# Reordering the instruction queues of a software-pipelined MoE and fast-weight stage

## Chip, cores and metric

One core of one Trainium2 chip runs the kernel. The metric is the device time of one execution in microseconds (us). The engines are named as in the profile: PE (TensorE, matmuls; PEld its weight loads), DVE (VectorE), ACT (ScalarE), POOL (GpSimd) and SP (SyncE).

## What is computed

A decoder of two layers on 64 sequences of 64 tokens with 128 channels, 4096 tokens in all. Only the third and fourth of its six steps matter here, layer 0's experts and layer 1's "attention", a fast-weight step:

```python
def _L0_ffn_ref(hidden_states, w_red, wg, W1, b1, W2, b2):     # 8 experts of 256, one per token
    gates = softmax((x @ w_red) @ wg_n.T); scores = max(gates); idx = argmax(gates)
    h = gelu((x @ W1[idx]) + b1[idx]); o = (h @ W2[idx] + b2[idx]) * scores

def _L1_attn_ref(...):               # 16 heads of 64; a sequence of 64 tokens is one chunk
    lr = sigmoid(xk @ theta + tb); eta = token_eta * (lr / HD)
    Z1 = xk @ W + bb; x_hat = (Z1 - mean) / std; y = g * x_hat + be
    gxh = (y - (xv - xk)) * g
    grad_x = (HD * gxh - gxh.sum() - x_hat * (gxh * x_hat).sum()) / (HD * std)
    Wn, bn = W - (eta * xk).T @ grad_x, bb - (eta * grad_x).sum()
    Zq = xq @ Wn + bn;  out = xq + g * (Zq - mean) / std + be;  return out @ wo

x = x + _L0_ffn_ref(_layernorm(x), ...)      # ln3, experts (moe0)
x = x + _L1_attn_ref(_layernorm(x), ...)     # ln4, fast weights (fw)
```

All is float32. The step before these two ends in a dense layer whose output (`dense_T`) the same stage of the kernel adds to x.

## The kernel before

The kernel runs three stages one after the other: a first one with two attentions and a recurrent layer (to about 1000 us of the span), the middle stage of this case (about 1001 to 1936 us), and a last one with attentions, a dense layer and experts. The change touches the middle stage alone, in `phase_c` from L2670 to L2940.

The 4096 tokens are eight groups g of 512, a group is four tiles t of 128 tokens. Each engine has its queue written out by hand as one loop over g from -1 to 8, and the helpers that it calls wait on semaphores by absolute count, so that an order on one engine can be changed by moving a line. The loop is a software pipeline: in period g the engines finish the output of group g-1 (y), do the fast weights of group g, and choose and run the experts of group g+1. A helper whose group is outside 0 to 7 does nothing.

In a period these parts follow one another, by the names of the helpers (their engine is the last word of the name):

- Start: `y_first_tensor` and `y_tensor` (L2214 to L2226, nine products into bank 6) finish group g-1. Meanwhile `sum_scalar` (L2102), `sum_back_tensor` (L2116) and `experts_added_vector` (L2125) bring the experts' sum of group g back to tokens and add it to x. ln4 follows: `moments_of` (L2140, L2143), `rstd_of` (L2150, L2152), `unit_of` (L2162), `turn_of` (L2170) and `fast_input_scalar` (L2179), which gives xT. `keep_gpsimd` (L2131) stores x.
- Rates: `rates_tensor` (L2186), `rates_in_vector` (L2194), `rates_exp_scalar` (L2200) and `rates_vector` (L2206 to L2210), the learning rates eta.
- Heads: 16 products `head_tensor` (L2428) over three banks, each copied by `head_scalar` (L2434): the queries and keys. A product waits until the one three before it is copied.
- Gradient of each tile t: `z_tensor` (L2441, L2442) makes Z1, `z_square_scalar` (L2461), `z_var_vector` (L2466) and `z_rstd_scalar` (L2471, L2474) its norm, `z_unit_vector` (L2486) x_hat. On POOL `gain_gpsimd` (L2504) multiplies it; `t_tensor` makes the target, `grad_vector` (L2513) adds the two, `grad_mean_vector` (L2518) and, behind POOL's `grad_unit_gpsimd` (L2523), `grad_dot_vector` (L2528) sum up, `grad_means_vector` (L2536) scales. `rate_vector` (L2544), `grad_less_mean_vector` (L2550), POOL's `grad_along_gpsimd` (L2556), `grad_less_vector` (L2563) and `step_vector` (L2569) finish the step. Two tiles share buffers in turn (t % 2).
- Query of each tile: `key_query_tensor` (L2583, banks 4 and 5) with the copy `key_query_scalar` (L2593); `zq_tensor` (L2441, L2442) and `zq_step_tensor` (L2616) accumulate Zq in banks 6 and 7; `zq_square_scalar` (L2627), `zq_var_vector` (L2632), `zq_rstd_scalar` and `zq_unit_vector` (L2644) normalise it; `zq_turn_tensor` (L2655, banks 4 and 5 again) and `zq_turned_scalar` (L2661) turn it. zq of tile t waits for zq_unit of tile t-1, as both use banks 6 and 7, and key_query of tile t (2 and 3) for the turned copy of tile t-2.
- Choice for group g+1: `hidden_gpsimd` (L2254) copies the dense output, `hidden_turn_tensor` (L2262) turns it, `hidden_added_vector` (L2271) adds it to x; ln3; `choice_input_scalar` (L2277), `choice_reduce_tensor` (L2282), `choice_reduced_scalar` (L2288), `choice_logits_tensor` (L2295), then small DVE instructions in `choice_best_vector` (L2303, L1917 to L1925, L2307), `choice_exp_scalar` (L2313), `choice_weights_vector` (L2319 to L2323) and `choice_parts_vector` (L2333, L2336).
- Experts of group g+1: `weights_turn_tensor` (L2349), `weights_turned_scalar` (L2358), `biases_tensor` (L2364), and for each of eight experts `weight_rows_tensor` (L2374), two `expert_input_tensor` (L2387), `expert_gelu_scalar` (L2397), `expert_weighted_vector` (L2405) and `expert_output_tensor` (L2413). An input product waits for the gelu two before it, an output product for its weighted hidden half, a row for the last use of the row before. Before the gelus ACT loads a table (L2109).

All the waits are in the helpers; those that the prediction's steps touch most are these (`at` is the count of the group):

```python
def key_query_tensor(pe, S, k, t):   # t 0: fw_heads_sb of all 16; t 1: fw_A of tile 0
        pe.wait_ge(S["fw_turned_sb"], at("fw_turned_sb", k, t - 1))      # t 2 and 3
def zq_tensor(pe, S, k, t):
        pe.wait_ge(S["fw_unit2"], at("fw_unit2", k, t))                  # t 1 to 3
def zq_step_tensor(pe, S, k, t):
    pe.wait_ge(S["fw_A"], at("fw_A", k, t + 1))
    pe.wait_ge(S["fw_step"], at("fw_step", k, t + 1))
```

Of the kernel before, what the change touches and what calls it, by code (L numbers as in the profile page):

```python
# [1729 lines left out]
def phase_c(m, w):  # L1730
# [937 lines left out]
    with ExitStack() as sems:  # L2668
        S = Signals(nc, sems)
        with nc.Block() as block:  # L2670
            @block.tensor
            def _(pe):
                for g in range(-1, GROUPS + 1):
                    y_first_tensor(pe, S, g - 1)
# [13 lines left out]
                    z_tensor(pe, S, g, 1)  # L2688
# [12 lines left out]
                    choice_logits_tensor(pe, S, g + 1)  # L2701
# [4 lines left out]
                    z_tensor(pe, S, g, 2)  # L2706
# [26 lines left out]
                    weight_rows_tensor(pe, S, g + 1, 1)  # L2733
                    expert_output_tensor(pe, S, g + 1, 0, 0)
                    expert_input_tensor(pe, S, g + 1, 2, 0)
                    expert_output_tensor(pe, S, g + 1, 0, 1)
                    expert_input_tensor(pe, S, g + 1, 2, 1)
                    expert_input_tensor(pe, S, g + 1, 3, 0)
                    expert_output_tensor(pe, S, g + 1, 1, 0)
                    weight_rows_tensor(pe, S, g + 1, 2)  # L2740
                    expert_input_tensor(pe, S, g + 1, 3, 1)
                    expert_output_tensor(pe, S, g + 1, 1, 1)
# [18 lines left out]
                    expert_output_tensor(pe, S, g + 1, 5, 0)
                    weight_rows_tensor(pe, S, g + 1, 7)
                    expert_output_tensor(pe, S, g + 1, 5, 1)
                    expert_output_tensor(pe, S, g + 1, 6, 0)
                    expert_output_tensor(pe, S, g + 1, 6, 1)
# [775 lines left out]
```

## Time and profile before

| what | us |
|---|---|
| median of 3 runs (lowest, highest) | 2452.38 (2451.78, 2454.27) |
| the profiled execution's own time | 2457.08 |
| its span in the profile | 2455.4 |
| busy in the span: PE, DVE, ACT, POOL | 2013.9, 1627.3, 1136.9, 687.3 |

The profiled execution is one run by itself: its time is 4.7 us above the median, and its span is 1.7 us shorter than its time. Busy shares are means over three stages with different limits, so a change in one stage is read from that stage's own rows: a table by stretch of time, the waits by engine and releaser, and the timeline of each engine in one period of the loop.

### The profile page before, as it was taken

To read this page: it belongs to the slowest core of one execution; us is meant where nothing else is said; L and a number is where in the kernel's file an instruction comes from. 1 tells how busy PE (TensorE), PEld (TensorE's weight loads), DVE (VectorE), ACT (ScalarE), POOL (GpSimd) and SP (SyncE) were. 2 spreads that over 40 slices of the span, in tenths; PEclk is the share of its full clock that TensorE was granted. 3 is DMA by queue.
4 is the path that set the end of the run, shared out by engine and by line. 5 is a ranking of instruction groups with operands and counts; after the bars stand their busy time and mean duration, and the time that the engine had idled before them with its cause. 6 is when DMAs were issued, how large, how long until landed. Compare 5 with 4: busy or idle time off the path is not lost. (4 is left out here: it accounts for less than half of the span.)

```text
span 2455.4 us, 38656 instructions
## 1 busy us (share of the span) xinstructions
PE 2013.9 (82%) x15025; PEld 1225.2 (50%) x15025; DVE 1627.3 (66%) x3304; ACT 1136.9 (46%) x1971; POOL 687.3 (28%) x425
## 2 busy tenths in 40 slices
PE   2677788778878998689999989898989558888897
PEld 1455565566556877344444444444444334444443
DVE  3587888878753545575849485766757357677673
ACT  1576677667643443244444444444444223444342
POOL 0574476457631001031415142222324100000000
PEclk9977777887677998799999999999999669999999
DMA  2000000000003200000000000000000000000000
GB/s 73 1 8 8 6 4 8 8 6 4 8 1 89 71 1 1 0 1 1 1 1 1 1 1 1 1 1 1 1 1 1 5 9 9 9 9 9 9 5 9
DMA packets 40533, 23.56 MB, mean 10 GB/s; under 512 B 17648, under 2 KB 36896, under 8 KB 40352
## 3 DMA queue, kind: packets, MB, share of 16 engines
q1 hardware_dynamic: 40352, 21.10, 3.2%
q8 instruction: 120, 1.97, 0.3%
q14 instruction: 61, 0.50, 0.1%
HBM read 18.99 MB, written 2.10 MB: 9 GB/s over the span
## 5 line engine op out<-in xcount | busy, mean ns | idle before, releaser
L2405 DVE TENSOR_TENSOR arena<-arena,lower_banks 128x512 f32<-128x512 f32 x128 | 84.4, 685 | 145.2 <-PE lower_banks L2374 99.9
L3001 ACT ACTIVATE arena<-lower_banks,moe_b 128x512 f32<-128x512 f32 x128 | 87.9, 686 | 135.9 <-PE lower_banks L2991 126.3
L449 ACT ACTIVATE arena<-upper_banks 128x512 f32<-128x512 f32 x192 | 107.4, 593 | 88.6 <-PE upper_banks L420 56.9
L2397 ACT ACTIVATE arena<-lower_banks,moe_b 128x512 f32<-128x512 f32 x128 | 87.1, 687 | 122.7 <-PE lower_banks L2413 94.1
L2387 PE MATMUL lower_banks<-hid_w,moe_w 128*128 128x512 f32 x256 | 140.0, 641 | 1.0 <-DVE fw_b L2486 1.0
L562 POOL TENSOR_TENSOR score_mha<-score_mha,row_max_mha 128x1024 f32<-128x1024 f32 x64 | 121.7, 1908 | 57.4 <-DVE row_max_mha L500 57.4
L420 PE MATMUL upper_banks<-ident,score_mha 128*128 128x128 f32 x512 | 109.6, 362 | 32.0 <-ACT arena L449 16.8
L2413 PE MATMUL lower_banks<-arena,moe_w 128*128 128x512 f32 x256 | 125.9, 593 | 0.0
L3017 PE MATMUL upper_banks<-arena,moe_w 128*128 128x512 f32 x256 | 124.6, 595 | 0.0
L2991 PE MATMUL lower_banks<-c_xT,moe_w 128*128 128x512 f32 x256 | 123.4, 599 | 0.0
L3010 DVE TENSOR_TENSOR arena<-arena,lower_banks 128x512 f32<-128x512 f32 x128 | 86.6, 683 | 49.6 <-ACT arena L3001 47.7
L420 PEld LDWEIGHTS upper_banks<-ident,score_mha 128*128 128x128 f32 x512 | 78.8, 185 | 70.0 <-issue 34.7
L2441 PE MATMUL upper_banks<-fw_zq,c_xT 128*128 128x512 f32 x128 | 76.7, 684 | 36.5 <-DVE fw_zq_sb L2644 36.5
L2131 POOL TENSOR_TENSOR x_all<-x_cur,fw_beo 128x512 f32<-128x512 f32 x8 | 10.2, 1278 | 343.7 <-DVE x_cur L2125 343.7
L2434 ACT ACTIVATE arena<-upper_banks 128x512 f32<-128x512 f32 x128 | 76.4, 597 | 50.5 <-PE upper_banks L2428 50.5
L490 POOL TENSOR_TENSOR score_lor<-causal,aux 128x1024 f32<-128x1024 f32 x32 | 90.6, 2831 | 3.8 <-ACT aux L538 3.8
L554 POOL TENSOR_TENSOR aux<-aux,score_lor 128x1024 f32<-128x1024 f32 x32 | 82.5, 2577 | 29.0 <-ACT aux L528 28.8
L546 ACT ACTIVATE score_mha<-score_mha 128x1024 f32<-128x1024 f32 x64 | 67.1, 1054 | 48.5 <-POOL score_mha L562 48.3
L2627 ACT ACTIVATE fw_sqq<-upper_banks 128x1024 f32<-128x1024 f32 x32 | 32.8, 1025 | 102.2 <-PE upper_banks L2616 101.9
L2387 PEld LDWEIGHTS lower_banks<-hid_w,moe_w 128*128 128x128 f32 x256 | 48.9, 205 | 58.5 <-issue 43.7
L500 DVE TENSOR_REDUCE row_max_mha<-score_mha 128x16 f32<-128x1024 f32 x64 | 77.1, 1214 | 1.1
L2413 PEld LDWEIGHTS lower_banks<-arena,moe_w 128*128 128x128 f32 x256 | 49.2, 192 | 54.3 <-issue 52.3
(465 smaller groups left out, 5233.2 us busy)
## 6 DMA issues: line engine op xcount, KB each, us to landing
ctx_cur<-in_ctx_dram SPq DMA_DIRECT2D x16, 256.0 KB, 3.0
moe_w<-in_L_ffn_W_dram SPq DMA_DIRECT2D x2, 1024.0 KB
out_dram<-arena SPq DMA_DIRECT2D x8, 256.0 KB, 2.4
arena<-in_mask_Bx1x1xS_ff_dram SPq DMA_DIRECT2D x16, 64.0 KB, 2.7
arena<-in_L_xattn_lstm_w_dram SPq DMA_DIRECT2D x1, 512.0 KB, 5.1
hid_w<-in_L_xattn_ffn_w_dram SPq DMA_DIRECT2D x2, 256.0 KB, 3.1
hid_w<-in_L_xattn_w_dram SPq DMA_DIRECT2D x2, 256.0 KB
fw_q<-in_L_attn_wq_dram SPq DMA_DIRECT2D x1, 512.0 KB
```

The lines of the kernel that those rows point to most:

```text
L420: tr = nc.tensor.transpose(pair[2][:, p * P:(p + 1) * P], score[stream][:, u % ring[stream], 2 * p:2 * p + 2, :], ident[:, :])
L449: nc.scalar.activation(PT[:, 4 * half:4 * half + 4, :], pair[2][:, 512 * half:512 * half + 512].rearrange("k (p q) -> k p q", p=4), ACT.Copy)\
L490: nc.gpsimd.tensor_tensor(sc, bcast(causal[:, :], 1, H), ax, ALU.subtract).then_inc(S["lor_masked"], 1)
L562: nc.gpsimd.tensor_tensor(sc, sc, bcast(row_max[stream][:, u % ring[stream], :], 2, SEQ), ALU.subtract)\
L2387: nc.tensor.matmul(bank(i % 2), w["moe0_w1"][:, e, c * P:(c + 1) * P], expert_xT, start=True, stop=True)\
L2397: nc.scalar.activation(expert_hid[:, e % 2, c, :], bank(i % 2), ACT.Gelu, bias=w["moe0_b1"][:, e, c:c + 1])\
L2405: nc.vector.tensor_tensor(expert_hid[:, e % 2, c, :], expert_hid[:, e % 2, c, :], bank(ROW_BANK), ALU.mult)\
L2413: nc.tensor.matmul(bank(SUM_BANK), w["moe0_w2"][:, i, :], expert_hid[:, e % 2, c, :], start=False, stop=(i == E * EC - 1)).then_inc(S["moe ...
L2991: nc.tensor.matmul(bank(i % 2), w["moe1_w1"][:, e, c * P:(c + 1) * P], xT[:, :], start=True, stop=True)\
L3001: nc.scalar.activation(plan.hid[:, e % plan.ring, c, :], bank(i % 2), ACT.Relu, bias=w["moe1_b1"][:, e, c:c + 1])\
L3010: nc.vector.tensor_tensor(hid, hid, bank(ROW_BANK), ALU.mult).then_inc(S["moe1_scaled"], 1)
L3017: nc.tensor.matmul(bank(4), w["moe1_w2"][:, i, :], plan.hid[:, e % plan.ring, c, :], start=False, stop=(i == E * EC - 1)).then_inc(S["moe1 ...
```

## The change

The diff moves lines within the four queues of the middle stage. No helper, tile, semaphore or count changes, and the last stage is the same text in both kernels. On PE:

```diff
 for g in range(-1, GROUPS + 1):
+    hidden_turn_tensor(pe, S, g + 1)
     y_first_tensor(pe, S, g - 1)
...
     y_tensor(pe, S, g - 1, (6, 7))
+    z_tensor(pe, S, g, 0)
     rates_tensor(pe, S, g)
-    z_tensor(pe, S, g, 0)
     y_back_tensor(pe, S, g - 1)
-    hidden_turn_tensor(pe, S, g + 1)
+    turn_of(pe, S, "ln3", g + 1, CHOICE_BANK)
     t_tensor(pe, S, g, 0)
     head_tensor(pe, S, g, 0)
+    z_tensor(pe, S, g, 1)
+    choice_reduce_tensor(pe, S, g + 1)
     head_tensor(pe, S, g, 1)
...
     t_tensor(pe, S, g, 1)
+    z_tensor(pe, S, g, 2)
     head_tensor(pe, S, g, 4)
+    choice_logits_tensor(pe, S, g + 1)
...
     head_tensor(pe, S, g, 15)
-    z_tensor(pe, S, g, 2)
     key_query_tensor(pe, S, g, 0)
...
     zq_step_tensor(pe, S, g, 1)
+    t_tensor(pe, S, g, 3)
     zq_turn_tensor(pe, S, g, 0)
-    t_tensor(pe, S, g, 3)
-    expert_input_tensor(pe, S, g + 1, 0, 0)
     key_query_tensor(pe, S, g, 2)
     zq_tensor(pe, S, g, 2)
     zq_step_tensor(pe, S, g, 2)
+    weights_turn_tensor(pe, S, g + 1)
     zq_turn_tensor(pe, S, g, 1)
-    weights_turn_tensor(pe, S, g + 1)
-    expert_input_tensor(pe, S, g + 1, 0, 1)
     key_query_tensor(pe, S, g, 3)
-    weight_rows_tensor(pe, S, g + 1, 0)
-    biases_tensor(pe, S, g + 1)
     zq_tensor(pe, S, g, 3)
     zq_step_tensor(pe, S, g, 3)
     zq_turn_tensor(pe, S, g, 2)
+    weight_rows_tensor(pe, S, g + 1, 0)
+    expert_input_tensor(pe, S, g + 1, 0, 0)
+    biases_tensor(pe, S, g + 1)
+    expert_input_tensor(pe, S, g + 1, 0, 1)
     zq_turn_tensor(pe, S, g, 3)
```

The 28 other expert products and seven rows behind that are interleaved in another order. On ACT:

```diff
     fast_input_scalar(act, S, g)
+    rstd_of(act, S, "ln3", g + 1)
     y_scalar(act, S, g - 1)
+    z_square_scalar(act, S, g, 0)
+    choice_input_scalar(act, S, g + 1)
     rates_exp_scalar(act, S, g)
-    z_square_scalar(act, S, g, 0)
     z_rstd_scalar(act, S, g, 0)
+    z_square_scalar(act, S, g, 1)
     head_scalar(act, S, g, 0)
+    z_rstd_scalar(act, S, g, 1)
...
+    choice_reduced_scalar(act, S, g + 1)
     head_scalar(act, S, g, 3)
+    z_square_scalar(act, S, g, 2)
     head_scalar(act, S, g, 4)
+    z_rstd_scalar(act, S, g, 2)
...
     head_scalar(act, S, g, 8)
+    choice_exp_scalar(act, S, g + 1)
...
     zq_square_scalar(act, S, g, 1)
+    zq_rstd_scalar(act, S, g, 1)
     zq_turned_scalar(act, S, g, 0)
-    zq_rstd_scalar(act, S, g, 1)
...
     zq_square_scalar(act, S, g, 2)
+    weights_turned_scalar(act, S, g + 1, 0)
     zq_turned_scalar(act, S, g, 1)
```

and the turned copy of tile 3 goes from behind the second gelu to ahead of the last. On DVE:

```diff
     experts_added_vector(dve, S, g)
+    hidden_added_vector(dve, S, g + 1)
     moments_of(dve, S, "ln4", g, x_cur, "moe0_added")
     unit_of(dve, S, "ln4", g, x_cur, "ln3", g)
+    moments_of(dve, S, "ln3", g + 1, x_next, "dense_added")
+    unit_of(dve, S, "ln3", g + 1, x_next, "ln4", g)
     rates_in_vector(dve, S, g)
+    z_var_vector(dve, S, g, 0)
+    y_added_vector(dve, S, g - 1)
+    z_unit_vector(dve, S, g, 0)
     rates_vector(dve, S, g)
...
     rate_vector(dve, S, g, 0)
     grad_vector(dve, S, g, 0)
+    z_var_vector(dve, S, g, 1)
     grad_mean_vector(dve, S, g, 0)
     z_unit_vector(dve, S, g, 1)
     grad_dot_vector(dve, S, g, 0)
     grad_means_vector(dve, S, g, 0)
+    rate_vector(dve, S, g, 1)
     grad_less_mean_vector(dve, S, g, 0)
     grad_vector(dve, S, g, 1)
+    z_var_vector(dve, S, g, 2)
+    grad_less_vector(dve, S, g, 0)
+    choice_best_vector(dve, S, g + 1)
+    grad_dot_vector(dve, S, g, 1)
+    z_unit_vector(dve, S, g, 2)
     grad_mean_vector(dve, S, g, 1)
     step_vector(dve, S, g, 0)
     grad_means_vector(dve, S, g, 1)
+    choice_weights_vector(dve, S, g + 1)
     grad_less_mean_vector(dve, S, g, 1)
+    choice_parts_vector(dve, S, g + 1)
     grad_less_vector(dve, S, g, 1)
...
     grad_means_vector(dve, S, g, 2)
+    z_unit_vector(dve, S, g, 3)
     grad_less_mean_vector(dve, S, g, 2)
-    rate_vector(dve, S, g, 3)
-    z_unit_vector(dve, S, g, 3)
     zq_var_vector(dve, S, g, 1)
...
     grad_dot_vector(dve, S, g, 3)
+    rate_vector(dve, S, g, 3)
     grad_means_vector(dve, S, g, 3)
+    zq_var_vector(dve, S, g, 2)
     grad_less_mean_vector(dve, S, g, 3)
-    zq_var_vector(dve, S, g, 2)
     zq_unit_vector(dve, S, g, 2)
```

(the lines that only leave their old place are left out of the DVE and ACT parts). On POOL:

```diff
-    keep_gpsimd(pool, S, g)
-    hidden_gpsimd(pool, S, g + 2)
     gain_gpsimd(pool, S, g, 0)
...
+    gain_gpsimd(pool, S, g, 2)
     grad_along_gpsimd(pool, S, g, 1)
-    gain_gpsimd(pool, S, g, 2)
...
     gain_gpsimd(pool, S, g, 3)
+    keep_gpsimd(pool, S, g)
     grad_unit_gpsimd(pool, S, g, 3)
+    hidden_gpsimd(pool, S, g + 2)
     grad_along_gpsimd(pool, S, g, 3)
```

## Rows read from the trace of the kernel before

**Rows 1.** Table by stretch: start:end, us, busy (instructions) PE, PEld, DVE, ACT, POOL, clock, DMA.
```profile
1389.80:1503.20 113.40, 104.91 (x786) 54.45 (x785) 78.72 (x111) 48.95 (x80) 32.77 (x14) 0.97 0.00 1
```

**Rows 2.** PE's waits, 1163 to 1843 us: us in all, times, longest.
```profile
PE upper_banks L2441 <- DVE fw_zq_sb L2644: 25.6, 12, 2.6
PE upper_banks L2655 <- DVE fw_zq_sb L2644: 19.2, 6, 3.2
```

**Rows 3.** Timeline of PE, one period: start, us, instruction, [idle before <- releaser].
```profile
1395.09 0.60 PE L2170 MATMUL lower_banks<-ident,x_norm 128*128 128x128 f32 x4
...
1440.16 1.60 PE L2441 MATMUL upper_banks<-fw_zq,c_xT 128*128 128x512 f32 x2 [2.63 <-DVE fw_zq_sb L2644]
...
1452.66 1.12 PE L2441 MATMUL upper_banks<-fw_zq,c_xT 128*128 128x512 f32 x2 [1.25 <-DVE fw_zq_sb L2644]
...
1463.09 1.02 PE L2441 MATMUL upper_banks<-fw_zq,c_xT 128*128 128x512 f32 x2
...
1467.41 1.09 PE L2655 MATMUL upper_banks<-ident,fw_zq_sb 128*128 128x128 f32 x8
1471.69 1.97 PE L2655 MATMUL upper_banks<-ident,fw_zq_sb 128*128 128x128 f32 x8 [3.19 <-DVE fw_zq_sb L2644]
...
1475.85 0.38 PE L2374 MATMUL lower_banks<-cwT_parts,sel 96*128 96x512 bf16 x1
...
1501.51 1.02 PE L2218 MATMUL upper_banks<-c_xT,fw_qo 128*128 128x512 f32 x2
```

**Rows 4.** Timeline of DVE in that period.
```profile
1398.24 0.22 DVE L2194 TENSOR_TENSOR fw_eta<-upper_banks,fw_theta_b 128x64 f32<-128x64 f32 x1 [4.51 <-PE upper_banks L2186]
...
1402.69 0.68 DVE L2271 TENSOR_TENSOR ctx_cur<-x_all,upper_banks 128x512 f32<-128x512 f32 x1
...
1404.53 0.86 DVE L2140 BATCH_NORM_STATS2 ln_stats<-ctx_cur 128x6 f32<-128x128 f32 x4
...
1405.59 1.49 DVE L2544 TENSOR_TENSOR fw_small<-fw_eta,fw_small 128x16 f32<-128x16 f32 x1
...
1410.67 1.11 DVE L2162 TENSOR_SCALAR x_norm<-ctx_cur,ln_moments,ln_rstd 128x128 f32<-128x128 f32 x4
...
1414.23 1.16 DVE L2536 TENSOR_SCALAR fw_small<-fw_small 128x32 f32<-128x32 f32 x1
...
1416.56 1.21 DVE L2513 TENSOR_TENSOR fw_o<-fw_gbe,lower_banks 128x1024 f32<-128x1024 f32 x1
...
1418.95 2.85 DVE L2563 TENSOR_TENSOR arena<-arena 128x1024 f32<-128x1024 f32 x1
...
1444.95 1.87 DVE L2544 TENSOR_TENSOR hid_w<-fw_eta,hid_w 128x16 f32<-128x16 f32 x1
...
1461.63 1.22 DVE L2644 TENSOR_TENSOR fw_zq_sb<-upper_banks,fw_small 128x1024 f32<-128x1024 f32 x1 [0.62 <-ACT fw_small L2474]
```

**Rows 5.** Timeline of DVE (first fence line) and POOL in the first stage.
```profile
317.96 1.42 DVE L481 SCALAR_TENSOR_TENSOR aux<-score_lor 128x1024 f32<-128x1024 f32 x1
...
318.26 3.34 POOL L554 TENSOR_TENSOR aux<-aux,score_lor 128x1024 f32<-128x1024 f32 x1
...
323.43 2.36 POOL L554 TENSOR_TENSOR aux<-aux,score_lor 128x1024 f32<-128x1024 f32 x1
```

**Rows 6.** Timeline of POOL in the period of rows 3.
```profile
1390.90 1.27 POOL L2131 TENSOR_TENSOR x_all<-x_cur,fw_beo 128x512 f32<-128x512 f32 x1 [42.35 <-DVE x_cur L2125]
1401.39 1.08 POOL L2254 COPY h_cur<-seq_x 128x512 f32<-128x512 f32 x1 [9.22 <-PE upper_banks L2262]
...
1415.46 2.94 POOL L2556 TENSOR_TENSOR arena<-arena,fw_small 128x1024 f32<-128x1024 f32 x1
```

**Rows 7.** Timeline of ACT in that period.
```profile
1447.34 1.02 ACT L2661 ACTIVATE arena<-upper_banks 128x1024 f32<-128x1024 f32 x1
```

**Rows 8.** Table by stretch, four us behind X in two periods.
```profile
1440.10:1444.10 4.00, 3.94 (x6) 1.27 (x6) 3.86 (x6) 0.78 (x3) 1.55 (x2) 0.57 0.00 0
1780.20:1784.20 4.00, 3.93 (x60) 2.46 (x62) 3.86 (x6) 0.78 (x3) 1.56 (x2) 1.00 0.00 0
```

More of the change, by code:

```diff
@@ L2732, in _ @@
                     expert_input_tensor(pe, S, g + 1, 1, 1)
-                    weight_rows_tensor(pe, S, g + 1, 1)
                     expert_output_tensor(pe, S, g + 1, 0, 0)
                     expert_input_tensor(pe, S, g + 1, 2, 0)
+                    weight_rows_tensor(pe, S, g + 1, 1)
                     expert_output_tensor(pe, S, g + 1, 0, 1)
                     expert_input_tensor(pe, S, g + 1, 2, 1)
+                    expert_output_tensor(pe, S, g + 1, 1, 0)
                     expert_input_tensor(pe, S, g + 1, 3, 0)
-                    expert_output_tensor(pe, S, g + 1, 1, 0)
                     weight_rows_tensor(pe, S, g + 1, 2)
+                    expert_output_tensor(pe, S, g + 1, 1, 1)
                     expert_input_tensor(pe, S, g + 1, 3, 1)
-                    expert_output_tensor(pe, S, g + 1, 1, 1)
+                    expert_output_tensor(pe, S, g + 1, 2, 0)
                     expert_input_tensor(pe, S, g + 1, 4, 0)
@@ L2750, in _ @@
                     expert_output_tensor(pe, S, g + 1, 3, 0)
+                    weight_rows_tensor(pe, S, g + 1, 4)
                     expert_input_tensor(pe, S, g + 1, 5, 1)
-                    weight_rows_tensor(pe, S, g + 1, 5)
                     expert_output_tensor(pe, S, g + 1, 3, 1)
@@ L2755, in _ @@
                     expert_output_tensor(pe, S, g + 1, 4, 0)
+                    weight_rows_tensor(pe, S, g + 1, 5)
+                    expert_output_tensor(pe, S, g + 1, 4, 1)
                     expert_input_tensor(pe, S, g + 1, 6, 1)
-                    expert_output_tensor(pe, S, g + 1, 4, 1)
+                    expert_output_tensor(pe, S, g + 1, 5, 0)
+                    weight_rows_tensor(pe, S, g + 1, 6)
+                    expert_output_tensor(pe, S, g + 1, 5, 1)
                     expert_input_tensor(pe, S, g + 1, 7, 0)
-                    weight_rows_tensor(pe, S, g + 1, 6)
+                    expert_output_tensor(pe, S, g + 1, 6, 0)
+                    weight_rows_tensor(pe, S, g + 1, 7)
                     expert_input_tensor(pe, S, g + 1, 7, 1)
[L2761 to L2764, printed above, removed]
                     expert_output_tensor(pe, S, g + 1, 6, 1)
@@ L2839, in _ @@
                     expert_gelu_scalar(act, S, g + 1, 7, 0)
+                    zq_turned_scalar(act, S, g, 3)
                     expert_gelu_scalar(act, S, g + 1, 7, 1)
@@ L2849, in _ @@
+                    z_unit_vector(dve, S, g, 0)
                     rates_vector(dve, S, g)
-                    y_added_vector(dve, S, g - 1)
-                    z_var_vector(dve, S, g, 0)
-                    hidden_added_vector(dve, S, g + 1)
-                    z_unit_vector(dve, S, g, 0)
-                    moments_of(dve, S, "ln3", g + 1, x_next, "dense_added")
                     rate_vector(dve, S, g, 0)
                     grad_vector(dve, S, g, 0)
+                    z_var_vector(dve, S, g, 1)
@@ L2857, in _ @@
                     grad_mean_vector(dve, S, g, 0)
-                    z_var_vector(dve, S, g, 1)
-                    unit_of(dve, S, "ln3", g + 1, x_next, "ln4", g)
                     z_unit_vector(dve, S, g, 1)
-                    rate_vector(dve, S, g, 1)
                     grad_dot_vector(dve, S, g, 0)
                     grad_means_vector(dve, S, g, 0)
+                    rate_vector(dve, S, g, 1)
                     grad_less_mean_vector(dve, S, g, 0)
                     grad_vector(dve, S, g, 1)
+                    z_var_vector(dve, S, g, 2)
@@ L2872, in _ @@
                     grad_less_mean_vector(dve, S, g, 1)
[L2873 removed]
+                    choice_parts_vector(dve, S, g + 1)
                     grad_less_vector(dve, S, g, 1)
[L2875 removed]
+                    rate_vector(dve, S, g, 2)
                     step_vector(dve, S, g, 1)
[L2877 to L2879 removed]
```

24 lines of the change are left out of this document (removed).

## The prediction

> **What bounds the kernel now.** The change reaches only the middle stage, so I read the table by stretch first: of a period of some 113 us, PE is busy 104.9 and DVE 78.7, at a granted clock of 0.97 [rows 1]. PE looks like the bound, but the list of PE's waits over six periods says what its pauses end on: the tile `fw_zq_sb`, which DVE writes in L2644, 25.6 and 19.2 us, 7.5 a period [rows 2]. In time order [rows 3] the period ends with the next y_first at 1501.51. Tile t's zq product can start only when DVE has finished zq_unit of tile t-1. These starts, which I call X, Y and Z, are 1440.16, 1452.66 and 1463.09; the last turn starts at 1471.69 after 3.19 us of idle. From the second row of experts (1475.85) to the end PE has no wait. So two stretches alternate: DVE sets the pace from about 1401 to 1463, PE sets it for the rest. An instruction moved on PE ahead of X, Y or Z gains nothing by itself; one that leaves the DVE stretch can.
>
> **The port between DVE and POOL** decides what a DVE instruction costs there. An elementwise DVE instruction with both inputs in SBUF took 1.22 us alone, but grad_less of tile 0 took 2.85, because gain and grad_unit ran on POOL [rows 4]. grad_vector of tile 1 (1416.56), which reads PSUM, took 1.21 while POOL's grad_along ran from 1415.46 [rows 4, 6]. The trace also shows who goes first when both want the port: L481 on DVE finished at 319.38, and the POOL instruction placed at 318.26 took 3.34 instead of 2.36 us [rows 5]. A DVE instruction that already waits goes ahead of POOL's next.
>
> **Start of a period: 0 us.** hidden_turn (0.43 us of PE) moves to the front, where it only fills; hidden_added (0.68), ln3's moments (1.06 from the start of L2140 to that of rate0) and ln3's unit (1.11, of which some 1.0 until the next one starts) go into DVE's 4.51 us idle ahead of rates_in [rows 4]. hidden_added now delays ln4 by 0.7 us, but ln4's turn at 1395.09 comes behind six y products [rows 3], about 1.4 us after its input; if that cover were gone the 0.7 would count whole.
>
> **DVE up to the means of tile 0: -0.8 us.** Of 2.76 us that leave, the moments lay under POOL's gain of tile 0: rate0 behind them took 1.49 us, held until 1407.08 [rows 4], and grad0 needs that gain in any case. The three rates instructions, ahead of z_var0 before (some 1.0 us), come in at this place. So until grad0 nothing is won, and I place it 0.2 us later. After it ln3's unit is missing, 1.0 us; grad_means0, held by gain1 until 1415.39 [rows 4], ends near 1414.6: -0.8.
>
> **From there to X: 0 to +1.2 us, taken +0.6.** The same work is in another order, with rate1 added. Before, the port cost 1.63 us on grad_less0 [rows 4], and by the same reading some 3.5 on the choice's small instructions. Now I count 1.9 on grad_less0, 1.35 on step0 (behind gain2), 1.6 on the choice weights (behind grad_along1): 4.9 against some 5.1. What the trace doesn't settle is rate1, put between means0 and grad_less_mean0. Before, grad_less_mean0 took the port at once and grad_along waited: 2.94 us, some 1.05 of it the wait [rows 6]. If POOL now gets in behind rate1, grad_less_mean0 waits out 1.9 us and X is 1.2 later. The Trainium skill, "SBUF — State Buffer", section "Who interferes with whom", says that issue order decides who blocks and the holder keeps the pair for its whole instruction; grad_less0's 2.85 us agrees. By that rule grad_along gets in and the whole +1.2 stands, which makes the final time about 2442. I take the middle, since no row shows this meeting.
>
> **X to Y: -1.1 us.** rate3 cost 1.87 us here, held by grad_along2 [rows 4]; it leaves. z_unit3, which reads PSUM, takes its place, and grad_less_mean2 then waits some 0.7 us for the same POOL instruction. Bounds: -1.7 (no wait) and +0.2 (if POOL's keep, 1.27 us [rows 6], got ahead of grad_less2). **Y to Z: -0.1 us.** grad_less_mean3 now stands behind grad_along3 (0.9), but it covers the 0.62 us that zq_unit2 waited for its rstd [rows 4]. Bounds -0.6 and +1.0 (the hidden copy, 1.08 us [rows 6], which moves behind grad_unit3).
>
> **PE in these stretches: 0 us.** New idle opens: key_query 0 comes right behind the last head and waits for its copy (about 0.85), and key_query 2 and 3 come right behind a turn and wait for ACT's 1.02 us copy [rows 7], as t_3 and two expert inputs no longer stand between. In ACT's queue, rstd of z2 and the choice's exponent stand ahead of later head copies, which holds the heads by 1 to 2.5 us. All ends before X, Y and Z by 0.4, 0.8 and 2.2 us in my count. The first is thin.
>
> **The tail: -0.75 us.** The expert inputs, weight row and biases that had filled other waits (0.86, 0.86, 0.22 and 0.96 us) now fill the 3.19 us ahead of the last turn, all but about 0.3. The wait itself ends no sooner: DVE and ACT still take 4.3 us from the last zq product. What goes is the clock's fall behind it: from the turn to the second row PE took 4.16 us. At the full clock it is 2.65: the turn before took 1.09 against 1.97, 0.93 until the next instruction starts, and an expert product takes 0.86 (28 of them and seven rows of 0.22 fill the 25.66 us from 1475.85 to 1501.51) [rows 3]. That is 1.5 us. But 2.2 us of idle ahead of Z is new. After 2.63 us of idle at X the granted clock was 0.57 over four us in this period, near the lower of its two levels (1.2 and 2.4 GHz), but 1.00 in another period after as long a wait [rows 8]. So half, between 0 and -1.5. The 25.66 us of experts stay; ACT's last turned copy (1.02) moves among the gelus, where ACT idles 1 to 2 us.
>
> **Once:** in the period before group 0, both first inputs move behind the row, and nothing hides them there: two products of 0.86 to 1.0 us, +1.8. In group 7, which has no experts behind it: -1. No DMA moves; SP's queue is empty in this stage.
>
> **Sum.** Seven periods of -0.8 + 0.6 - 1.1 - 0.1 - 0.75 = -2.15 give -15.1; with +1.8 and -1, -14.3. The profiled execution took 2457.08 us (span 2455.4), so 2442.8; against the median of 2452.38, 4.7 lower, **2438**. With the near ends of the two open terms (+1.2 and clock 0) it is 7 x -0.8 + 0.8 = -4.8, 2448; with the far ends (0 and -1.5), 7 x -3.5 + 0.8 = -23.7, 2429.
>
> **Rivals.** (a) *POOL first*: slower. keep and the hidden copy now stand in the middle of POOL's queue. If POOL's next instruction took the port ahead of a waiting DVE one, grad_less2 would lose 1.27, rate3 and grad_less_mean3 1.08, and grad_less_mean0 the 1.2: -2.0 + 3.5 = +1.5 each period, no tail gain as Z's idle grows, 7 x 1.5 + 1.8 = +12.3: 2465. It decides from 1.7 us of such losses a period on. Against it: [rows 5]. Chance 0.16. (b) *PE or ACT late at X*: the head copies wait longer than I count. With 2 us more, X is 1.6 later: 7 x (-2.15 + 1.6) + 0.8 = -3, 2449; with 3.5 us more, 2460. For it: 0.4 us of slack. Chance 0.17. (c) *All moved DVE work counts*: -2.76 and -1.5 a period, if POOL's gain0 also starts earlier than I count: 7 x -4.26 + 0.8 = -29: 2423. Against it: gain0 is needed either way. Chance 0.12. That the change doesn't do what it says has no room: it touches no last-stage line, and the orders are plain.
>
> **Numbers.** The forecast (0.55) has its own range 2429 to 2448. A measurement of this kernel can tell about 0.2%, 4.9 us, from no change: faster means under 2447.5. All but 0.02 of the forecast and all of (c) lie there: 0.65. Of (b), 0.11 is the same and 0.06 slower; with the forecast's upper end, same is 0.13; slower, with (a), 0.22. The range 2424 to 2458 leaves out most of (a) and half of (c).
>
> **What would show it.** Right: the period falls from 113 to near 111; PE's wait before the last turn falls from 3.2 to under 0.6; its wait at X shrinks from 2.63 to under 1, and waits of 1 to 2 us appear before key_query 2 and 3. rate3's 1.87 is gone, and step0 and grad_less_mean2 are longer than 1.22. Wrong: grad_less2 behind keep; PE, and not DVE, last at X; a low clock after Z in every period; a wait inside the experts.

## The result and the profile after

The changed kernel took **2419.05 us** (2417.10 to 2421.42, four runs), the kernel before beside it 2452.30 (2451.78 to 2454.27): a ratio of 0.9861 [0.9849, 0.9873], 33 us less. The direction was forecast; the size was more than twice the 14.3 us of the sum, and the time lies below the range that began at 2424. The profiled execution took 2421.42 us with a span of 2419.7, 35.7 shorter than the span before.

Where the 35.7 us went can be read from VectorE's timeline alone, if one cuts each period at the same instructions: from experts_added (L2125) to the start of the first grad_vector (L2513), to the second one, and to the ends of the four zq_unit (L2644), which release TensorE. Means over the seven full periods, each worked out from those rows, and the last period (group 7, no experts) up to the start of its y_added (L2246):

| kernel | period | to grad 0 | to grad 1 | to unit 0 | to unit 1 | to unit 2 | to unit 3 | tail | last |
|---|---|---|---|---|---|---|---|---|---|
| before | 113.39 | 17.14 | 9.41 | 23.55 | 12.49 | 10.28 | 8.81 | 31.71 | 92.55 |
| after | 108.73 | 16.35 | 8.29 | 22.48 | 11.15 | 10.38 | 9.80 | 30.28 | 89.64 |
| difference | -4.66 | -0.79 | -1.12 | -1.07 | -1.34 | +0.10 | +0.99 | -1.43 | -2.91 |

7 x -4.66 - 2.91 = -35.5, all but 0.2 of the change of the span. Four stretches of VectorE each gave about a microsecond, the tail gave 1.4, and 1.0 was lost between the third and fourth unit.

The table by stretch, one period of the changed kernel (start:end, us, busy PE, PEld, DVE, ACT, POOL, clock, DMA):
```profile
1374.50:1483.50 109.00, 102.73 (x784) 53.63 (x783) 77.03 (x110) 47.65 (x79) 32.55 (x14) 0.98 0.00 1
```
PE's waits in it and five other periods, 1160 to 1840 us (us in all, times, longest):
```profile
PE upper_banks L2583 <- ACT arena L2661: 14.7, 12, 1.3
PE upper_banks L2441 <- DVE fw_zq_sb L2644: 14.2, 12, 2.1
...
PE upper_banks L2655 <- DVE fw_zq_sb L2644: 2.4, 6, 0.4
```
Against [rows 1] the period is 4.4 us shorter with the same work (784 matmul rows in place of 786). Against [rows 2] the wait for VectorE at the last turn fell from 19.2 to 2.4 us, that at X, Y and Z from 25.6 to 14.2; new are 14.7 us for ACT's copy ahead of key_query 2 and 3. PE's timeline of that period shows where they lie:
```profile
1424.05 1.13 PE L2441 MATMUL upper_banks<-fw_zq,c_xT 128*128 128x512 f32 x2
...
1432.86 1.16 PE L2583 MATMUL upper_banks<-arena 64*64 64x64 f32 x64 [1.15 <-ACT arena L2661]
1434.67 1.13 PE L2441 MATMUL upper_banks<-fw_zq,c_xT 128*128 128x512 f32 x2 [0.64 <-DVE fw_zq_sb L2644]
...
1441.62 1.16 PE L2583 MATMUL upper_banks<-arena 64*64 64x64 f32 x64 [1.28 <-ACT arena L2661]
1444.89 1.12 PE L2441 MATMUL upper_banks<-fw_zq,c_xT 128*128 128x512 f32 x2 [2.10 <-DVE fw_zq_sb L2644]
...
1446.07 1.82 PE L2441 MATMUL upper_banks<-fw_zq,c_xT 128*128 128x512 f32 x2
...
1455.14 1.10 PE L2655 MATMUL upper_banks<-ident,fw_zq_sb 128*128 128x128 f32 x8 [0.41 <-DVE fw_zq_sb L2644]
```
The first row is X: it has no wait, so PE is now later than VectorE there, where it waited 2.63 us in [rows 3]. The wait at Z (1444.89) is 2.10 us, and right behind it the next two matmuls of the same shape take 1.82 in place of 1.02 to 1.13: the clock fell there. The table by stretch, four us behind Z in three periods, shows that it falls in some periods only:
```profile
1229.43:1233.43 4.00, 3.94 (x59) 2.42 (x61) 2.25 (x2) 0.00 (x0) 0.00 (x0) 1.00 0.01 4
...
1444.96:1448.96 4.00, 4.00 (x20) 1.62 (x22) 2.23 (x2) 0.00 (x0) 0.00 (x0) 0.65 0.00 0
...
1661.42:1665.42 4.00, 4.00 (x10) 1.54 (x11) 2.25 (x2) 0.00 (x0) 0.00 (x0) 0.60 0.00 0
```
In four of seven periods the way from unit 2 to unit 3 took 10.1 to 11.6 us, in the other three 8.78, as before: that is the +0.99 of the table. The wait at Z was 2.10 us in five of the seven; in the other two the clock had already fallen at Y, behind the wait of 0.64, which made unit 1 to unit 2 take 10.77 in place of 10.22 and the wait at Z 0.97.

VectorE's timeline of the period holds the meetings on the port:
```profile
1386.72 0.23 DVE L2194 TENSOR_TENSOR fw_eta<-upper_banks,fw_theta_b 128x64 f32<-128x64 f32 x1 [2.51 <-PE upper_banks L2186]
1386.98 1.22 DVE L2466 TENSOR_REDUCE fw_small<-arena 128x16 f32<-128x1024 f32 x1
...
1399.73 0.16 DVE L2544 TENSOR_TENSOR hid_w<-fw_eta,hid_w 128x16 f32<-128x16 f32 x1
1399.85 1.22 DVE L2550 TENSOR_TENSOR arena<-arena,fw_small 128x1024 f32<-128x1024 f32 x1
...
1410.98 2.47 DVE L2569 TENSOR_TENSOR arena<-arena,fw_small 128x1024 f32<-128x1024 f32 x1
...
1428.19 2.00 DVE L2550 TENSOR_TENSOR arena<-arena,fw_small 128x1024 f32<-128x1024 f32 x1
...
1431.23 2.25 DVE L2563 TENSOR_TENSOR arena<-arena 128x1024 f32<-128x1024 f32 x1
```
and POOL's timeline its other side:
```profile
1399.90 2.94 POOL L2556 TENSOR_TENSOR arena<-arena,fw_small 128x1024 f32<-128x1024 f32 x1
...
1410.02 2.35 POOL L2504 TENSOR_TENSOR arena<-arena,fw_g 128x1024 f32<-128x1024 f32 x1 [4.87 <-DVE arena L2486]
...
1429.06 3.34 POOL L2504 TENSOR_TENSOR fw_gbe<-fw_b,fw_g 128x1024 f32<-128x1024 f32 x1
1432.36 2.26 POOL L2131 TENSOR_TENSOR x_all<-x_cur,fw_beo 128x512 f32<-128x512 f32 x1
```
grad_less_mean 0 (1399.85) took its plain 1.22 us and POOL's grad_along 0, 0.05 us behind it, took 2.94: VectorE was first. step 0 (1410.98) waited out gain 2, as forecast. grad_less_mean 2 (1428.19) waited for grad_along 2 and then went ahead of gain 3 (3.34 us, 1.0 more than it takes alone). grad_less 2 (1431.23) went ahead of keep (2.26 in place of 1.27).

### The profile page after: what moved, and what is told of

It reads as the page before. It is cut to its first block and busy times, and to the rows that moved or that the text cites. A ratio compares the mean times of both kernels' runs of the same rounds, so it can differ in the third digit from the quotient of the medians.

```text
span 2419.7 us, 38656 instructions
## 1 busy us (share of the span) xinstructions
PE 1988.5 (82%) x15025; PEld 1213.8 (50%) x15025; DVE 1617.9 (67%) x3304; ACT 1130.2 (47%) x1971; POOL 685.2 (28%) x425
## 5 line engine op out<-in xcount | busy, mean ns | idle before, releaser
L2504 POOL TENSOR_TENSOR arena<-arena,fw_g 128x1024 f32<-128x1024 f32 x16 | 37.6, 2349 | 491.8 <-DVE arena L2486 491.8
L2387 PE MATMUL lower_banks<-hid_w,moe_w 128*128 128x512 f32 x256 | 130.3, 596 | 0.0
L2434 ACT ACTIVATE arena<-upper_banks 128x512 f32<-128x512 f32 x128 | 73.6, 590 | 14.4 <-PE upper_banks L2428 14.3
```

The costliest lines, as they stand in the source:

```text
L2387: nc.tensor.matmul(bank(i % 2), w["moe0_w1"][:, e, c * P:(c + 1) * P], expert_xT, start=True, stop=True)\
```

## The experiments

The theory after the result: VectorE's stretches gave the time, because its chains now start earlier; the fillers moved to the tail gave theirs too. The rivals: the choice's new place gave it, or the tail alone, or the clock.

**Parts of the change one at a time: the choice's front, the tail's fillers.** In the kernel before, these five steps moved to the front, VectorE's as the change has them (the lines at their old places are left out):
```diff
+hidden_turn_tensor(pe, S, g + 1)
 y_first_tensor(pe, S, g - 1)
...
+rstd_of(act, S, "ln3", g + 1)
...
 experts_added_vector(dve, S, g)
+hidden_added_vector(dve, S, g + 1)
 moments_of(dve, S, "ln4", g, x_cur, "moe0_added")
 unit_of(dve, S, "ln4", g, x_cur, "ln3", g)
+moments_of(dve, S, "ln3", g + 1, x_next, "dense_added")
+unit_of(dve, S, "ln3", g + 1, x_next, "ln4", g)
 rates_in_vector(dve, S, g)
```


> The kernel before, with one part of the change: hidden_turn first on PE, hidden_added, the ln3 moments and the ln3 unit behind the ln4 unit on DVE, the ln3 rstd behind the ln4 input on ACT; all else in the old order. Theory 'DVE work': the 2.76 us that leave the DVE stretch count nearly whole, X comes 2.0 to 2.8 us earlier in the period, and the kernel takes 7 x -2.4 = -17 us: 2435. Rival 'order': the moments lay under POOL's gain and only the unit counts (the step of the prediction), X comes about 0.8 to 1.0 earlier, 7 x -0.9 = -6 us: 2446, and the rest of the gain is in how the DVE instructions of two tiles are interleaved.

Measured: 2454.87, ratio 0.9996 [0.9987, 1.0005]: nothing. DVE's waits in it, 1160 to 1840 us, say why:
```profile
DVE arena L2513 <- POOL arena L2504: 14.7, 6, 2.5
DVE x_norm L2162 <- ACT ln_rstd L2152: 11.6, 12, 1.3
...
DVE fw_b L2486 <- ACT hid_w L2474: 3.7, 6, 0.6
```
VectorE had 1.7 us less to do ahead of the first gradient and 1.0 less behind it. Ahead of the gradient it waits 2.5 us for POOL's gain 0 instead; behind it z_unit 1 now waits 0.6 us for its rstd. Emptying VectorE's queue alone gave nothing, as the prediction's sentence on gain 0 had it: grad 0 starts 17.02 us behind experts_added in six of seven periods, with this order and before, the means of tile 0 come 0.31 earlier, and the tail takes 0.32 longer. Both theories missed. The reverse, the changed kernel with that front back at its old places on all engines (with the choice's turn, reduce and logits on PE):

> The changed kernel with that part undone, and with it the choice's steps on PE and ACT up to its exponent back at their old places among the heads; tiles' order, tail and POOL as changed. 'DVE work': 7 x +2.4 = +17 us on 2419: 2436. 'Order': +0.9 a period, +6: 2425.

Measured: 2471.64, ratio 1.0061 [1.0046, 1.0076], some 50 us above the changed kernel. The first unit came 6.6 us later in a period. Both theories missed, and the run is confounded: its early choice_best on VectorE waits for logits that PE now makes late.
```profile
DVE choice L2303 <- PE upper_banks L2295: 25.4, 6, 4.8
```
It shows only that these orders go together: an instruction left late on one engine stops the next engine's whole queue.

The tail's four fillers alone, in the kernel before:
```diff
 zq_turn_tensor(pe, S, g, 2)
+weight_rows_tensor(pe, S, g + 1, 0)
+expert_input_tensor(pe, S, g + 1, 0, 0)
+biases_tensor(pe, S, g + 1)
+expert_input_tensor(pe, S, g + 1, 0, 1)
 zq_turn_tensor(pe, S, g, 3)
```


> The kernel before, with the first row, the two inputs of expert 0 and the biases moved between the turns of tiles 2 and 3 on PE. Theory 'clock': the wait before the last turn falls from 3.2 to some 0.4 us and the stretch behind it runs at the full clock, but PE now idles 2 to 3 us ahead of Z; if the clock stays up there, -1.5 us a period, -10: 2442; if it falls there each time, 0 to -2: 2451. Rival 'place of the work': those four products were not free at their old place, and their leaving lets X to Z come earlier: more than -1.5 a period, under 2440, with Z minus Y below 10.2.

Measured: 2449.36, ratio 0.9968 [0.9956, 0.9981]. The tail fell from 31.71 to 29.90 us, and unit 2 to unit 3 rose from 8.81 to 9.34 (in the profiled execution, which at 2439.29 us was the fastest of the seven: its first experts_added starts 7.6 us earlier, which these segments leave out). And those four taken back in the changed kernel:

> The changed kernel with these four products back at their old places: inputs ahead of key_query 2 and 3, row and biases behind key_query 3. 'Clock': the wait before the last turn is 3.2 us again and costs its 1.5 us, while the waits ahead of key_query 2, 3 and Z are filled and no clock falls at Z (it fell in about half of the periods of the changed kernel): +0.7 to +1.5 a period, +5 to +10: 2424 to 2429. 'Place of the work': Y or Z later by over 0.5 us in each period, and more than +12: over 2431.

Measured: 2421.53, ratio 0.9861 [0.9845, 0.9878], the same as the changed kernel. Up to unit 2 all segments are equal to 0.2 us; then unit 3 takes 8.78 (no fall behind Z) and the tail 31.92 (a fall behind the last turn): 40.71 in sum beside 40.08. The last turn of this run, in PE's timeline:
```profile
1443.67 1.12 PE L2441 MATMUL upper_banks<-fw_zq,c_xT 128*128 128x512 f32 x2 [0.88 <-DVE fw_zq_sb L2644]
...
1452.46 1.94 PE L2655 MATMUL upper_banks<-ident,fw_zq_sb 128*128 128x128 f32 x8 [3.20 <-DVE fw_zq_sb L2644]
```
With the fillers ahead of Z its wait is 0.88 us and the full clock stays; the 3.20 us of idle are at the turn, and the turn runs at the low clock (1.94 for 1.10). So inside the change the tail's part only moved the fall from one place to the other, for a net gain near nothing; in the kernel before it was worth 1.3 us a period (-1.81 and +0.53), because the fall behind Z came less often there (two periods of seven).

**The order at the start of a period.** The changed kernel with PE's rates ahead of z of tile 0 again:
```diff
+rates_tensor(pe, S, g)
 z_tensor(pe, S, g, 0)
-rates_tensor(pe, S, g)
```


> The changed kernel with one call moved back: TensorE multiplies for the rates ahead of z of tile 0 again, as before the change; all other orders stay new. In the changed kernel the first gradient step (grad_less_mean of tile 0's predecessor, line 2513 in the first place of a period) starts 16.23 us after experts_added, before the change 17.02. Theory A (that 0.79 was won on TensorE, because z of tile 0 no longer stands behind the rates' multiply and VectorE gets its squares' mean earlier): the first gradient starts near 17.0 again, every full period is about 0.8 longer, and 7 of them make some 5.6 us, about 2425 beside 2419. Theory B (it was won on VectorE alone, which takes y_added and the rates in another order and ln3 earlier): first gradient stays at 16.2, time within 1.5 us of the changed kernel.

Measured: 2433.52, ratio 0.9921 [0.9907, 0.9935]. The first gradient starts 17.08 us behind experts_added in six of seven periods, where it was 16.23: theory A, 0.85 us, but the time rose by 14, not 6. VectorE's timeline of this run has z_var 0 waiting for ACT's square of the late z:
```profile
1393.96 1.22 DVE L2466 TENSOR_REDUCE fw_small<-arena 128x16 f32<-128x1024 f32 x1 [3.08 <-ACT arena L2461]
```
The rest is mostly the clock: unit 2 to unit 3 took 10.2 to 11.6 us in all seven periods, 1.03 more in the mean.

**The choice's second half at its old places**, on VectorE and ScalarE:
```diff
-choice_best_vector(dve, S, g + 1)
 grad_dot_vector(dve, S, g, 1)
...
 grad_means_vector(dve, S, g, 1)
-choice_weights_vector(dve, S, g + 1)
+choice_best_vector(dve, S, g + 1)
 grad_less_mean_vector(dve, S, g, 1)
-choice_parts_vector(dve, S, g + 1)
+choice_weights_vector(dve, S, g + 1)
 grad_less_vector(dve, S, g, 1)
 rate_vector(dve, S, g, 2)
+choice_parts_vector(dve, S, g + 1)
```


> The changed kernel with the expert choice's second half back at its places of before: on VectorE the best of the logits behind the second gradient's mean, the weights behind grad_less_mean of tile 1, the parts behind rate2, and on ScalarE the choice's exponent behind the activation of expert part 15. From the second gradient's start to the end of the first zq_unit the changed kernel takes 1.07 us less than before; the itemised steps of VectorE say that the choice's three instructions came down from 6.5 to 4.9 us in sum and the rest gave half a microsecond back. Theory A (the place of these instructions gave it: in the new place they meet no POOL instruction on the port): first zq_unit 1.0 to 1.2 us later in each period, 8 times, about 2428. Theory B (the earlier start of POOL's and TensorE's work around tile 1 gave it, and the choice would be as quick at its old place): within 1.5 us of the changed kernel.

Measured: 2419.00, ratio 0.9861 [0.9848, 0.9875]: theory B. All segments equal those of the changed kernel within 0.02 us; one of the small instructions pays for grad_along 1 at either place (1.68 us of L1919 here, 1.69 of L2323 there). With z_unit 2 and gain 2 put back as well:
```diff
-z_unit_vector(dve, S, g, 2)
 grad_mean_vector(dve, S, g, 1)
...
 step_vector(dve, S, g, 1)
+z_unit_vector(dve, S, g, 2)
+rate_vector(dve, S, g, 2)
+choice_parts_vector(dve, S, g + 1)
...
-gain_gpsimd(pool, S, g, 2)
 grad_along_gpsimd(pool, S, g, 1)
+gain_gpsimd(pool, S, g, 2)
```


> The changed kernel with the stretch between the second gradient and the first zq_unit put back to the order of before: the choice's second half as in the run with the late choice (which cost nothing), and z_unit 2 behind step 1, rate 2 and the choice's parts behind it, and on POOL gain 2 behind grad_along 1. In the changed kernel POOL's gain 2 meets step 0 on the port, which takes 2.47 us in place of 1.14; before the change it met the choice's parts, one of whose instructions took 2.26 in place of 0.19. Theory A (the earlier z_unit 2 gave the 1.07 us that this stretch takes less: gain 2 meets a long VectorE instruction rather than a row of short ones, and grad 2 finds it ready): first zq_unit 0.8 to 1.1 us later, 8 times, 2425 to 2428. Theory B (this order isn't what gave it; z of tile 2 is there earlier in any order): within 2 us of the changed kernel.

Measured: 2432.36, ratio 0.9905 [0.9890, 0.9920]. The second gradient to unit 0 took 23.37 us, 0.89 more than in the changed kernel: theory A. Of the 1.70 us by which its period is longer the other 0.8 are the clock behind Z again (six of seven periods). So 0.9 of the 1.07 come from the earlier z_unit 2 and gain 2 (moved together here, with rate 2 and the parts behind step 1): gain 2 meets step 0 (1.3 us lost) and not the choice's parts (2.07 lost). These parts, and the other choice instruction that paid, are in VectorE's timeline of the kernel before:
```profile
1424.82 1.68 DVE L1919 TENSOR_TENSOR choice<-choice,choice_small 128x32 f32<-128x32 f32 x1
...
1433.81 2.26 DVE L2336 TENSOR_TENSOR cw_rest<-choice,cw_parts 128x32 f32<-128x32 f32 x1
```

**The first part on all engines, alone, in the kernel before**: the new orders of PE, ACT and VectorE up to grad_less_mean 0. With ln3 and the hidden turn as in the first run, its core on PE and VectorE is:
```diff
+z_tensor(pe, S, g, 0)
 rates_tensor(pe, S, g)
-z_tensor(pe, S, g, 0)
...
+y_added_vector(dve, S, g - 1)
 z_unit_vector(dve, S, g, 0)
+rates_vector(dve, S, g)
...
 grad_vector(dve, S, g, 0)
+z_var_vector(dve, S, g, 1)
 grad_mean_vector(dve, S, g, 0)
...
 grad_means_vector(dve, S, g, 0)
+rate_vector(dve, S, g, 1)
```


> The kernel before with the first part of the new orders alone, on all engines: hidden_turn first in the period, z of tile 0 ahead of the rates on TensorE and its mean ahead of y_added and the rates on VectorE, z of tile 1 behind head 0, ln3's moments and unit early, the mean of z1 ahead of grad_mean 0, rate 1 behind the means of tile 0. From the means of tile 1's gradient on, and in the tail, everything stays as before. In the kernel before the first zq_unit ends 49.98 us after experts_added, the second gradient starts at 26.43. Theory A (the gain up to the second gradient, 1.9 us a period in the changed kernel, comes from this part alone, since VectorE's chain starts earlier at TensorE's first z): second gradient at 24.5, first zq_unit near 48.1, 8 times 1.9 = 15 us less, about 2437. Theory B (the change's parts hang together: the heads of TensorE and the choice that stay late hold VectorE's choice, as when the choice's front alone was moved): first zq_unit at 49 to 50, time 2445 to 2453.

Measured: 2437.65, ratio 0.9929 [0.9916, 0.9941]: theory A to a microsecond. Grad 0 at 16.19, grad 1 at 24.44, unit 0 at 48.00, with the old order untouched from there on. This part, at which the prediction put 0.8 us, gives 2.1 up to unit 0, and by itself 18 of the 33 us.

**rate 3 back behind grad_less_mean 2:**
```diff
 grad_less_mean_vector(dve, S, g, 2)
+rate_vector(dve, S, g, 3)
...
-rate_vector(dve, S, g, 3)
```


> The changed kernel with rate_vector of tile 3 moved back right behind grad_less_mean of tile 2 on VectorE, its place before the change; nothing else moves. It puts the same question of the shared port that the prediction left undecided (a short VectorE instruction that is ready while POOL's next one waits for the port too): POOL's gain for tile 3 starts in the changed kernel as soon as grad_less_mean of tile 2 ends, and VectorE's rate3 would stand there too. Theory A (VectorE's next instruction gets the port first, as grad_less_mean of tile 0 did in the changed kernel): rate3 takes 0.16 and everything to Y is later by 0.1 to 0.2 us in a period, about 1 us in all, some 2420. Theory B (POOL's gain goes first, as before the change, where rate3 took 1.87 us, 1.7 of it waiting): Y is later by 1.3 to 2.3 us in a period, and 8 of them make the time 2429 to 2437.

Measured: 2424.89, ratio 0.9887 [0.9873, 0.9900]. VectorE's timeline of this run, and then POOL's:
```profile
1428.20 1.99 DVE L2550 TENSOR_TENSOR arena<-arena,fw_small 128x1024 f32<-128x1024 f32 x1
1430.12 2.32 DVE L2544 TENSOR_TENSOR hid_w<-fw_eta,hid_w 128x16 f32<-128x16 f32 x1
```
```profile
1427.22 1.90 POOL L2556 TENSOR_TENSOR arena<-arena,fw_small 128x1024 f32<-128x1024 f32 x1 [2.43 <-DVE fw_small L2536]
1429.08 3.33 POOL L2504 TENSOR_TENSOR fw_gbe<-fw_b,fw_g 128x1024 f32<-128x1024 f32 x1
```
On the meeting theory B is right: the port went from grad_along 2 to the waiting grad_less_mean 2, then to the waiting gain 3, and only then to rate 3, which took 2.32 us for its 0.16. Unit 1 is 1.24 later. On the sum both theories missed: the period grew by 0.97 only. The clock stayed up behind Z in six of seven periods (0.82 us less on unit 3); it fell ahead of Y instead, where PE now waits 3.40 us in place of 1.15 for the turned copy ahead of key_query 2, and unit 2 took 0.55 more. PE's timeline of this run:
```profile
1435.12 1.99 PE L2583 MATMUL upper_banks<-arena 64*64 64x64 f32 x64 [3.40 <-ACT arena L2661]
```

**Towards a better version.** One filler of the tail put ahead of Z, the other three left between the turns:
```diff
+expert_input_tensor(pe, S, g + 1, 0, 0)
 zq_tensor(pe, S, g, 3)
...
-expert_input_tensor(pe, S, g + 1, 0, 0)
```


> The changed kernel with one of TensorE's four fillers put elsewhere: the first input multiply of expert 0 goes ahead of zq 3 (in front of Z) in place of between turns 2 and 3; router row 0 and the biases stay between the turns. In the changed kernel TensorE waits 2.1 us at Z and 0.4 before the last turn, and in 4 of 7 periods the granted clock is at its lower level behind Z, where the way to the fourth zq_unit takes 10.25 us in place of 8.78; with all four fillers in front of Z taken away from the turns the fall stood behind the last turn, and the tail took 31.9 in place of 30.3. Theory A (the fall comes with the longest idle stretch of TensorE, and two middle ones bring none): no fall at either place, every period 107.5, time 2411 to 2415. Theory B (one instruction of 1.2 us is too little at one of the two places): fall in some periods at Z or behind the last turn, time 2417 to 2423.

Measured: **2408.85** (2405.14 to 2415.36), ratio 0.9823 [0.9809, 0.9837]: faster than both kernels, and its interval and the changed kernel's do not meet. PE's waits, 1160 to 1840 us:
```profile
PE upper_banks L2441 <- DVE fw_zq_sb L2644: 9.1, 11, 1.1
PE upper_banks L2655 <- DVE fw_zq_sb L2644: 7.5, 6, 1.3
```
The table by stretch, four us behind Z and four behind the last turn, one period of it:
```profile
1331.56:1335.56 4.00, 3.94 (x61) 2.42 (x63) 2.21 (x2) 0.00 (x0) 0.00 (x0) 1.00 0.01 4
...
1341.26:1345.26 4.00, 4.00 (x11) 1.74 (x11) 1.29 (x3) 2.07 (x4) 0.00 (x0) 1.00 0.00 0
```
No wait is over 1.3 us, and the clock is at 1.00 at both places in all seven full periods. Unit 2 to unit 3 takes 8.77 to 8.79 us in every full period, and the tail 29.94 to 30.34. Of the 10.4 us by which this run's span is below the changed kernel's, 6.2 lie between the first experts_added and the last y_added; 3.8 lie ahead of the middle stage, in code that is the same, and are not the filler's. And with zq_unit 1 ahead of grad_less 2 on top:
```diff
 zq_var_vector(dve, S, g, 1)
-grad_less_vector(dve, S, g, 2)
 zq_unit_vector(dve, S, g, 1)
+grad_less_vector(dve, S, g, 2)
```


> The run with the split fillers (2408.85) with one more exchange on VectorE: zq_unit of tile 1 ahead of grad_less of tile 2. In the changed kernel grad_less 2 takes 2.25 us (1.0 of it waiting for POOL's gain 3) ahead of zq_unit 1, and TensorE waits 0.64 us for that unit at Y and 2.1 at Z. Theory A (Y and Z are set by the order of these two alone): Y comes up to 0.6 us earlier, where TensorE becomes the bound, and Z too: 8 times 0.6 = 5 us less, about 2404. Theory B (POOL's keep now gets the port ahead of grad_less 2, which stands behind zq_unit 1, and step 2 and the way to Z are as late as before): Y 0.6 earlier, Z the same or up to 0.7 later, time 2408 to 2415.

Measured: 2415.95, ratio 0.9838 [0.9825, 0.9852]. Unit 1 ends 1.45 us earlier and unit 2 takes 1.49 longer: theory B. The stage takes 844.97 us in its profile beside 844.59 in that of the run before it (from the first experts_added to the last y_added); the 5 us between their starts (1051.07 and 1045.66) lie ahead of the stage, in code that is the same. The exchange gives nothing that can be told: the two ratios' intervals overlap.

## Why the prediction was wrong

The bound was read rightly: VectorE sets the pace up to Z, PE behind it, and each stretch had its term. But the exchange of z of tile 0 and the rates on PE had no term of its own, by the prediction's sentence that "an instruction moved on PE ahead of X, Y or Z gains nothing by itself", and that is the step that failed first. Four sizes were off, all in the same direction but one.

- **"Until grad0 nothing is won, and I place it 0.2 us later": -0.79.** The step took VectorE's own order for what binds. [Rows 4] had 4.51 us of idle ahead of rates_in; what grad 0 waits for is a chain that starts on PE. A row of PE's timeline that I passed over has it, in the kernel before:
```profile
1397.24 0.96 PE L2186 MATMUL upper_banks<-fw_lr,c_xT 128*128 128x16 f32 x8
1398.05 1.10 PE L2441 MATMUL lower_banks<-fw_z,c_xT 128*128 128x512 f32 x2
```
The rates stood 0.81 us in front of z of tile 0. In the changed kernel z_var 0 (1386.98) comes 1.1 us after z's last matmul, with the rates behind it, and with the rates put back the 0.85 are lost. VectorE's new order was needed as well. In the kernel before, y_added stood ahead of z_var 0 and waited for PE itself, and z_var 0 came right behind it, just as the square of the late z was done (1400.49 and 1.03 us on ACT):
```profile
1400.93 0.69 DVE L2246 TENSOR_TENSOR x_all<-x_all,upper_banks 128x512 f32<-128x512 f32 x1 [1.07 <-PE upper_banks L2239]
1401.55 1.22 DVE L2466 TENSOR_REDUCE fw_small<-arena 128x16 f32<-128x1024 f32 x1
```
So PE's exchange alone should have left z_var 0 where it was; that was not run.
- **The means of tile 0: -0.8 in all, measured -2.0** (-0.79, and -1.19 from grad 0 to the means: 7.08 against 5.89, from the starts of L2513 and L2536). The 1.0 for ln3's unit came true with z_var 1 ahead of grad_mean 0; in the first run, where z_var 1 stayed behind it, only 0.31 of it did. What failed is the sum's starting point, the 0.2 us by which grad 0 was to be late.
- **"0 to +1.2 us, taken +0.6" up to X: measured -1.0** (+0.08 to grad 1, -1.07 from there). The meeting that the prediction left open did not happen: rate 1 took 0.16 us, grad_less_mean 0 was at the port 0.05 us ahead of POOL's grad_along 0, which then took 2.94 us. The rule of the Trainium skill, "SBUF — State Buffer", section "Who interferes with whom", on which the 2442 was reckoned, says that issue order decides; the trace agrees with it, and it was my reading of who issues first that was wrong. The rest, -1.07, is for the most part the port account, worked out at 4.9 against 5.1: read off VectorE's timelines it was 4.5 (grad_less 0 1.8, step 0 1.2, the choice's weights 1.5) against 5.2 (1.6, the best's 1.5, the parts' 2.1). What counted was the choice's parts: behind an early z_unit 2 they meet no POOL instruction, and the loss on step 0 that stands for it is less than the 2.07 they lost. The run with that order put back gave 0.89 of it back.
- **X to Y, -1.1: measured -1.34** from unit 0 to unit 1, inside its bounds. rate 3 was the cause, shown by moving it back (+1.24). **Y to Z, -0.1: +0.10.**
- **The tail, -0.75: measured -1.43 on the tail and +0.99 at Z, -0.44 in sum.** The mechanism was named ("2.2 us of idle ahead of Z is new"; measured 2.10), the even odds were close (the fall came in four periods of seven), and the term was near.
- **Once, +1.8 and -1:** the last period measured -2.91, since the steps up to X count there too. The +1.8 came out as +1.4: from the stage's first hidden copy on POOL (L2254 at 1001.01 before, 999.77 after) to the first experts_added (1049.61 and 1049.79) it took 48.60 us before, 50.01 after and 48.50 in the run without the tail's fillers. It hardly shows in the span, as this execution's first stage ended 1.2 us earlier, in code that is the same.

In the sum the forecast's -2.15 a period came out as -4.66: the two steps up to X account for 2.8 of the 2.5 that it was short (-0.8 and +0.6 forecast, -2.0 and -1.0 measured), the rest of the terms for +0.3 against it. Rival (c), 2423 at 0.12, had the size but the wrong reason: VectorE's moved work by itself gives no time (the first run). Rival (a) is excluded by keep's 2.26 us. Rival (b) came true in its sign, X 0.6 us behind the end of unit 0 and without a wait, but not in its price: unit 0 itself came 2.97 us earlier, and in the run with the old window, where PE waits at X again, unit 0 to unit 1 takes the same 11.16 us. The step on PE had counted 0.4 us of slack there. Of the signs named, right were the last turn (0.41), X, the waits of 1.15 and 1.28 ahead of key_query 2 and 3, step 0 and grad_less_mean 2; the period fell to 107.5 to 109 in six of seven (111.1 in the first), not 111, and PE, not VectorE, is last at X, which I had listed as a sign of loss: a sign has to name the time too, not only who is last.

## What to carry to other kernels

Before an idle stretch is called cover, follow its releaser back to the engine where its chain starts: here 0.8 us of products ahead of that first one cost their whole length, under 4.5 us of idle on the next engine, and it took a new order in both queues to win them. Where two engines share a port, move the short instructions away from a long partner, and count who arrives first, not how much there is to do. Idle time that can't be removed may be worth splitting: here two waits of 1.1 and 1.3 us kept the clock up in every full period, where one of 2.1 or 3.2 us let it fall in most.

## What the runs showed of the hardware

- The port was handed on to whoever stood waiting, in turn: grad_along 2, grad_less_mean 2, gain 3, rate 3 in the run with rate 3 back. A VectorE instruction of 0.16 us right behind one that took the port from POOL paid 2.2 us. The prediction's [rows 5] had only the first half of this.
- After waits of 2.10 us at Z the granted clock over the next four us was 0.50 to 0.66, at or near its lower level (0.50 is 1.2 of 2.4 GHz), in three of the five full periods of the changed kernel that had such a wait, and in all five with the rates first. In the two other full periods of each kernel the clock had fallen to 0.57 at Y, behind waits of 1.15 us at key_query 2 and 0.64 at Y, and the wait at Z was only 0.97; it fell again there in one of the two and in both. After 0.6 to 1.0 us at Z in the runs without the tail's fillers and with rate 3 back it fell in one of fourteen. After 3.2 us at the last turn it fell in all seven periods without the tail's fillers, and in five of seven with the first part alone. After 1.05 and 1.26 us at the two places, in the run with the split fillers, it fell in none.
- So the length of one wait does not decide by itself. What does stays open; it was not tried. With the rates first, a change of 0.85 us a period cost 14 us in all, so a part's price can't be read from the time alone, only from its own segment.
